# Moving work between engines and places ahead of and inside the first steps of a two-layer recurrent memory

## The reference, cut to what matters

```
k = l2norm(x_t @ Wk); v = x_t @ Wv; q = l2norm(x @ Wq)      # block 1: a memory that learns
for t in 16 steps:                                          # x_t: the 4x16 tokens of image row t
    g = grad of mean((mlp(params, k) - v)**2)               # mlp: h + gelu(h @ w1) @ w2, twice
    mom = eta * mom - lr * g
    params = params * (1 - forget) + mom                    # eta, lr, forget: means of sigmoids of x_t
out = mlp(mean over batch of params, q)                     # the read-out
y = sum over top-2 experts of weight * (gelu(ln(x) * ln_g[e] @ W1[e]) @ W2[e])   # block 2, 8 experts
A[..., 16i:16i+16] = conv1x1(A, w1) + b1, four times        # block 3, its first chain ("conv-1")
h, c = lstm step over 256 tokens                            # block 4
```

## Time and profile before

| what | value |
|---|---|
| median of the runs | 546.06 us |
| the profiled execution | 546.64 us, its span 544.8 us |
| PE busy | 476.3 us (87%) |
| DVE busy | 293.7 us (54%) |
| ACT busy | 224.3 us (41%) |
| POOL busy | 99.8 us (18%) |
| mean granted clock of PE | 0.986 |

### The profile page before, as it was taken

The page is one execution under the profiler, slowest core; times in us unless marked ns, Lnnn a source line. Parts: engine busy times, 40 slices in busy tenths (PEclk is TensorE's granted clock), DMA queues, the critical chain, the costliest instruction groups (busy, mean ns, idle before and its releaser), DMA issues.

```text
span 544.8 us, 11175 instructions
## 1 busy us (share of the span) xinstructions
PE 476.3 (87%) x3945; PEld 295.2 (54%) x3952; DVE 293.7 (54%) x1382; ACT 224.3 (41%) x1118; POOL 99.8 (18%) x101
## 2 busy tenths in 40 slices
PE   7899999999999998988887999778888887888886
PEld 4588888888865234855543776333333333333333
DVE  2966666666666756056556444664444444444443
ACT  2365556555525741025533344333333333333332
POOL 4287777767510000000000000000000000000000
PEclk8999999999997999999999999999999999999999
DMA  7600000000000000000000000000000000000000
GB/s 223 271 0 2 2 1 0 2 1 2 0 2 0 1 2 0 1 1 2 2 2 1 1 2 1 2 1 1 2 1 2 1 0 2 2 1 2 2 2 19
DMA packets 3081, 7.68 MB, mean 14 GB/s; under 512 B 1484, under 2 KB 2065, under 8 KB 2833
## 3 DMA queue, kind: packets, MB, share of 16 engines
q1 hardware_dynamic: 3026, 6.97, 3.8%
HBM read 6.71 MB, written 0.26 MB: 13 GB/s over the span
## 4 chain that ended last, share of the span: by engine, by line
PE 54%; DVE 22%; ACT 16%; issue 8%; DMA 0%; DVEq 0%; ACTq 0%
PE bk L700 12%; DVE bk L1491 8%; ACT gi L1050 6%; DVE mem L1494 6%; ACT bk L1054 6%; PE bk L659 6%; PE bk L340 3%; PE bk L585 2%; PE bk L508 2%; PE bk L838 2%; PE bk L603 2%; PE bk L489 2%; PE bk L467 2%; PE bk L477 2%; PE bk L392 2%
## 5 line engine op out<-in xcount | busy, mean ns | idle before, releaser
L838 PE MATMUL bk<-idle 128*64 128x512 bf16 (+1 forms) x650 | 175.7, 371 | 0.0
L700 PEld LDWEIGHTS bk<-mem,lvh 65*64 65x64 f32 x1536 | 79.9, 136 | 144.3 <-DVE mem L1494 142.5
L700 PE MATMUL bk<-mem,lvh 65*64 65x4 f32 x1536 | 102.1, 205 | 45.5 <-DVE mem L1494 45.1
L1050 ACT ACTIVATE gi<-bk 128x4 f32<-128x4 f32 x256 | 44.9, 175 | 136.7 <-PE bk L700 136.3
L1491 DVE TENSOR_TENSOR_SCAN bk<-gi 64x12 f32<-64x12 f32 x256 | 47.6, 186 | 91.1 <-ACT gi L1050 88.7
L1494 DVE SCALAR_TENSOR_TENSOR mem<-og,bk 64x4 f32<-64x4 f32 x256 | 38.5, 150 | 53.7 <-ACT bk L1054 53.7
L838 PEld LDWEIGHTS bk<-idle 128*64 128x64 bf16 x650 | 55.3, 110 | 16.1 <-issue 2.4
L1054 ACT ACTIVATE bk<-bk 64x4 f32<-64x4 f32 x256 | 36.6, 143 | 45.2 <-DVE bk L1491 45.2
L1498 DVE SCALAR_TENSOR_TENSOR gi<-mem,bk 64x4 f32<-64x4 f32 x255 | 39.1, 153 | 8.8
L1052 ACT ACTIVATE og<-bk 64x4 f32<-64x4 f32 x256 | 42.6, 167 | 0.0
L1140 DVE TENSOR_TENSOR mem<-mem,bk 128x256 f32<-128x256 f32 x64 | 27.0, 421 | 17.2 <-PE bk L385 11.4
(11 more groups left out here) (317 smaller groups left out, 743.7 us busy)
## 6 DMA issues: line engine op xcount, KB each, us to landing
cw<-in_cw SPq DMA_DIRECT2D x1, 3456.0 KB, 12.2
w<-in_w SPq DMA_DIRECT2D x1, 520.0 KB
mem<-in_memw SPq DMA_DIRECT2D x1, 512.0 KB, 3.6
w1g<-in_w1g SPq DMA_DIRECT2D x1, 512.0 KB
w<-in_w SPq DMA_DIRECT2D x1, 512.0 KB
xm<-in_xm SPq DMA_DIRECT2D x1, 256.0 KB, 2.7
xs<-in_x SPq DMA_DIRECT2D x1, 256.0 KB, 3.9
out<-xs SPq DMA_DIRECT2D x1, 256.0 KB, 2.0
```

Of the source, the lines that this page charges most:

```text
L700: return nc.tensor.matmul(bk[row:row + D, 2 * (s // CH % 2) + k, c:c + B], lvh[:, g, :], hist[:, s, :], start=False, stop=True, skip_group ...
L838: nc.tensor.matmul(bk[64:128, 1, 0:n], idle[:, 0:D], idle[:, 128:128 + n], start=True, stop=True)
L1050: nc.scalar.activation(gi[:, 2:2 + 3 * B:3], bk[:, bank, cols], ACT.Tanh).then_inc(sem("in_gate"), 1)
```

## The change

1. POOL no longer multiplies `w1g`. ACT does it in eight pieces of 128x128, one at the end of each of the steps 3 to 10.
2. On DVE the masked keys `kblk` are computed ahead of the unit queries `QV`, and the gate sums (`gsum`, `glin`) move from ahead of the loop into step 0, behind `v_sub`. There `gram` is masked ahead of the rates.
3. On PE in step 0, `a1` comes right behind `h1`; `gram` and then the gate sums come behind `a1`. The queries are transposed two tiles at a time in the steps 1 to 4, behind `grad_w10`, and ACT copies them to `qq` in front of that step's second gelu.
4. The three products of the conv-1 chain and their copies move to the read-out; with them the two groups of fillers in the front shrink from five to two and from five to three.
5. POOL's `k_rows(0)` moves behind the first rate products; blocks 4 to 7 go into the steps 1 to 4.

The diff, cut to its core:

```
-            pool.wait_ge(sem("ld_w1"), 64)
-            nc.gpsimd.tensor_tensor(w1g[:, :, :], w1g[:, :, :], wide(lng[:, :], 128), ALU.mult).then_inc(sem("w1g"), 1)
...
-            k_rows(0)
...
-            for n in range(1, NT):
+            for n in range(4):
                 k_rows(n)
...
+                if t <= 4:
+                    k_rows(t + 3)
...
-            nc.tensor.matmul(bk[0:D + 1, 0, 0:D + 1], c1p[:, 2, :], c1last[:, :], start=True, stop=True).then_inc(sem("c1_ps"), 1)
-            busy(5, 1)
...
+            busy(2, 1)
             pe.wait_ge(sem("KK"), 1)
...
-            busy(5, 3)
+            busy(3, 3)
...
+                if 1 <= t <= 4:
                     pe.wait_ge(sem("QV"), 1)
+                    if t == 1:
+                        pe.wait_ge(sem("rates"), 1)
+                    else:
+                        pe.wait_ge(sem("qq"), t - 1)
+                    for n in range(2):
+                        ins = nc.tensor.transpose(bk[:, 7, 256 + n * 128:384 + n * 128], QV[:, 2 * t - 2 + n, :], ident)
+                    ins.then_inc(sem("qqT_ps"), 1)
...
+            nc.tensor.matmul(bk[0:D + 1, 2, 0:D + 1], c1p[:, 2, :], c1last[:, :], start=True, stop=True).then_inc(sem("c1_ps"), 1)
             pe.wait_ge(sem("FW"), 4)
...
+            pe.wait_ge(sem("c1"), 1)
+            nc.tensor.matmul(bk[0:D + 1, 3, 0:D + 1], c1p[:, 1, :], c1a[:, :], start=True, stop=True).then_inc(sem("c1_ps"), 1)
             pe.wait_ge(sem("ld_w1"), 64)
...
+            pe.wait_ge(sem("c1"), 2)
+            nc.tensor.matmul(bk[0:D + 1, 2, 0:D + 1], c1p[:, 0, :], c1b[:, :], start=True, stop=True).then_inc(sem("c1_ps"), 1)
             busy(AFTER[1], 7)
...
+                if 1 <= t <= 4:
+                    act.wait_ge(sem("qqT_ps"), t)
+                    nc.scalar.copy(qq[:, :].rearrange("p (b t c) -> p t b c", b=B, t=T)[:, 4 * t - 4:4 * t, :, :],
+                                   bk[:, 7, 256:512].rearrange("p (t b c) -> p t b c", t=4, b=B)).then_inc(sem("qq"), 1)
                 act.wait_ge(sem("a1"), t + 1)
...
+                if 3 <= t < 3 + E:
+                    e = t - 3
+                    if e == 0:
+                        act.wait_ge(sem("ld_w1"), 64)
+                    ins = nc.scalar.activation(w1g[:, e, :], w1g[:, e, :], ACT.Copy, scale=lng[:, e:e + 1])
...
             table(ACT.Sqrt)
+            act.wait_ge(sem("c1_ps"), 2)
+            nc.scalar.copy(c1b[:, :], bk[0:D + 1, 3, 0:D + 1]).then_inc(sem("c1"), 1)
             root(2)
...
+            inverse(1, 1)
+            unit(KK[:, :, 0:D], 1)
+            unit(KK[:, :, D:2 * D], 1).then_inc(sem("KK"), 1)
+            inverse(2, 0)
             dve.wait_ge(sem("ld_id"), 16)
...
+            unit(QV[:, :, 0:D], 0)
+            unit(QV[:, :, D:2 * D], 0).then_inc(sem("QV"), 1)
```

More of the change, by code:

```diff
@@ L327, in _ @@
             pool.wait_ge(sem("f_y"), 2)
-            pool.wait_ge(sem("w1g"), 1)
             nc.gpsimd.memset(W3, 0.0).then_inc(sem("zeros3"), 1)
@@ L376, in _ @@
             pe.wait_ge(sem("gS"), 2)
-            nc.tensor.matmul(bk[0:D + 1, 2, 0:D + 1], c1p[:, 0, :], c1b[:, :], start=True, stop=True).then_inc(sem("c1_ps"), 1)
-            busy(5, 3)
+            busy(3, 3)
             def grad_w11(t):
@@ L458, in _ @@
                 else:
-                    pe.wait_ge(sem("qq"), 2)
+                    pe.wait_ge(sem("vneg"), 2)
+                    pe.wait_ge(sem("QV"), 1)
+                    for n in range(NT):
+                        w = min(128, (T - 1 - 2 * n) * TB)
+                        ins = nc.tensor.matmul(bk[:, 6 - n // 4, n % 4 * 128:n % 4 * 128 + w], kblk[:, n * 128:(n + 1) * 128],
+                                               kblk[:, (2 * n + 1) * TB:(2 * n + 1) * TB + w], start=True, stop=True)
+                        if n % 4 == 3:
+                            ins.then_inc(sem("gram_ps"), 1)
+                    pe.wait_ge(sem("ld_g"), 32)
+                    pe.wait_ge(sem("glin"), 1)
+                    for g in range(3):
+                        ins = nc.tensor.matmul(bk[:, 7, 256 + g * B * T:256 + (g + 1) * B * T], gsel[:, g, :], glin[:, :],
+                                               start=True, stop=True)
+                    ins.then_inc(sem("gate_ps"), 1)
                 for p in range(2):
@@ L566, in _ @@
             ins.then_inc(sem("logit_ps"), 1)
+            pe.wait_ge(sem("c1"), 3)
             pe.wait_ge(sem("XT"), 2)
@@ L575, in _ @@
             pe.wait_ge(sem("x2A"), 2)
+            pe.wait_ge(sem("w1g"), 1)
             pe.wait_ge(sem("ld_w2"), 32)
@@ L931, in _ @@
                     ins.then_inc(sem("R1"), 1)
+                if 3 <= t < 3 + E:
[3 more added lines that the diff above has]
+                    ins = nc.scalar.activation(w1g[:, e, :], w1g[:, e, :], ACT.Copy, scale=lng[:, e:e + 1])
+                    if e == E - 1:
+                        ins.then_inc(sem("w1g"), 1)
             for n in range(2):
@@ L942, in _ @@
             nc.scalar.copy(b1p[:, :], bk[:, 4, 0:E * HC]).then_inc(sem("b1p"), 1)
+            act.wait_ge(sem("c1_ps"), 3)
+            nc.scalar.copy(c1a[:, :], bk[0:D + 1, 2, 0:D + 1]).then_inc(sem("c1"), 1)
             root(3)
@@ L1168, in _ @@
                 if t == 0:
+                    dve.wait_ge(sem("ld_g"), 32)
+                    dve.wait_ge(sem("gS"), 2)
+                    link(nc.vector.tensor_reduce(gsum[:, :], gS[:, :].rearrange("p (s c) -> p s c", c=C), AX, ALU.add))
+                    nc.vector.tensor_scalar(glin[:, :], gsum[:, :], gaff[:, 0:1], gaff[:, 1:2], ALU.mult, ALU.add).then_inc(sem("glin"), 1)
+                    for n in range(2):
+                        dve.wait_ge(sem("gram_ps"), n + 1)
+                        nc.vector.tensor_tensor(gram[:, 8 * n + 1:8 * n + 9 - n, :],
+                                                bk[:, 6 - n, 0:(8 - n) * TB].rearrange("p (t c) -> p t c", c=TB), mid(mg, 8 - n),
+                                                ALU.mult).then_inc(sem("gram"), 1)
                     dve.wait_ge(sem("gate_ps"), 1)
@@ L1184, in _ @@
                     ins.then_inc(sem("lr"), 1)
-                    for n in range(2):
-                        dve.wait_ge(sem("gram_ps"), n + 1)
-                        nc.vector.tensor_tensor(gram[:, 8 * n + 1:8 * n + 9 - n, :],
-                                                bk[:, 6 - n, 0:(8 - n) * TB].rearrange("p (t c) -> p t c", c=TB), mid(mg, 8 - n),
-                                                ALU.mult).then_inc(sem("gram"), 1)
                 dve.wait_ge(sem("q0"), t + 1)
```

49 lines of the change are left out of this document (6 added, 43 removed).

## The result

| | before | changed |
|---|---|---|
| median of ten runs each | 546.33 us | 550.24 us |
| lowest to highest | 545.37 to 549.75 | 547.17 to 551.42 |
| profiled execution, its span | 546.64, 544.8 us | 551.08, 549.3 us |
| mean granted clock in it | 0.986 | 0.975 |

The changed kernel is slower: ratio 1.0056, 95% interval 1.0032 to 1.008. The forecast was 545.9 with an upper end of 547.8. Executions of one kernel differ by some us, and they differ with the mean clock: among 23 runs of the kernel before beside the first experiments, those at 0.985 to 0.99 took 545.9 to 548.0 us, those at 0.969 to 0.973 took 552.0 to 553.6.

A forecast was written before the change was run, and what follows sets the result against it. No engine alone bounds it, but the wait ending last in each place (PE 54% of the chain). Step 0 -1.2 to -1.5, steps 1 to 4 +1.0, read-out +0.15: middle -0.2, median forecast 545.9 us, range 543.5 to 547.8.

The forecast's parts named there:

- I take **+0.15** in all: Read-out: first conv-1 product +0.12 on PE's chain, the other two and their copies 0 to 0.15 more.
- the forecast's own signs of being wrong: Masked keys later than 20 us, steps 1 to 4 as long as the others, or steps 3 to 10 growing 0.3 us.
- Front: Up to the masked keys: clamp 1.36 to 0.17 us, masked keys complete at 19.15 in place of 21.84.
- Step 0's chain: Step 0 up to the masked prediction: it starts near 27.9 in place of 30.30, with PE at 2.4 GHz.
- the -2.4: Step 0: masked prediction 2.4 us earlier than the profiled 30.30, if PE runs at 2.4 GHz.
- The gain of the front thus passes, and nothing is added: Step 0: the front's 2.69 us carries through as -2.4; DVE's longer chain refills the wait freed by removed transposes.
- `kblk` ahead of `QV` (-1.20): Front on DVE: the masked keys start where `QV` started, 19.36 in place of 20.56, 1.20 us earlier.
- the forecast -1.2 to -1.5: End of step 0: 1.2 to 1.5 us earlier, with one stretch of about 3 us at 1.2 GHz.
- Step 0's clock: Step 0: one stretch of about 3 us at 1.2 GHz, on `gram` (-1.2, not -2.4) or the back part (0.9 lost).
- The rival "slower than before": Step 0: PE at 1.2 GHz in `gram` and again in the back part; sum +0.85, 546.9 us, chance 0.22.
- Steps 1 to 4: Two query transposes a step on PE paid in full, 0.23 each step: +1.0 us (0.9 to 1.4).
- What costs nothing: `w1g` pieces on ACT in idle time before the first gelu, and `k_rows` within POOL's waits: no cost.

The follow-up runs named there:

- run 3: Changed kernel with the conv-1 chain taken out of the read-out and put into PE's wait of step 0: 550.96 us, ratio 1.008.
- run 1: Changed kernel with the `w1g` multiplication back on POOL ahead of the loop: 549.94 us, ratio 1.0051.
- run 10: Changed kernel with ten fillers in PE's wait of step 0, and 16 fillers replacing the left-out `b1p` products in the read-out: 544.49 us, ratio 0.9924.
- run 2: Changed kernel with the query transposes in steps 5 to 8 in place of 1 to 4: 554.13 us in a single execution.
- 6: Changed kernel with the `b1p` products left out of the read-out and 16 fillers in their place: 547.94 us, ratio 0.9961.
- 7: Kernel before with the `b1p` products left out of the read-out and 16 fillers in their place: 545.23 us, ratio 0.9944.
- 9: Changed kernel with ten fillers in step 0 where PE waits 2.50 us for DVE: 547.79 us, ratio 1.0011.
- run 12: Kernel before with the `b1p` products of experts 4 to 7 behind the expert weights' transposes, 8 fillers for them: 546.97 us, ratio 0.9974.
- 13: Changed kernel with ten fillers in step 0's wait, two `b1p` products in each of steps 5 to 12, 16 fillers in the read-out: 549.19 us, ratio 1.0035.
- 14: Kernel before with two `b1p` products in each of steps 5 to 12 and 16 fillers in the read-out: 548.74 us, ratio 1.0.
- 15: Changed kernel, ten step-0 fillers; `b1p` products at the loop's end and behind the expert weights' transposes, 16 read-out fillers: 546.98 us, ratio 1.0013.
- 16: Kernel before with `b1p` products at the loop's end and behind the expert weights' transposes, 16 read-out fillers: 547.13 us, ratio 1.0.
- run 4: Kernel before with only the conv-1 chain, three products and copies, moved to the read-out: 551.76 us, ratio 1.0068.
- run 8: Changed kernel with the `b1p` products moved into PE's wait of step 0 and 16 fillers in their place in the read-out: 551.95 us, ratio 1.0031.

## Why the prediction was wrong

The step that failed is the read-out: "I take **+0.15** in all". It priced three products in PE's instruction time and never asked for the clock in that place. It measured +4.15, and run 3, with PE's old read-out and the same 17 us at 1.2 GHz, has 3.79 of it: nearly all is the clock, about 17 us at 1.2 GHz in place of 7. The profile before already showed the two short stretches there; I had read the windows of step 0 alone. None of the forecast's own signs of being wrong looked at the read-out, and none of them came true.

- **Front**: right. Clamp 0.17 us, masked keys at 18.93 for 19.15. That DVE stands behind POOL's product is shown by run 1.
- **Step 0's chain**: right as a mechanism. `gram` ran at 2.4 GHz and the masked prediction came at 27.51 (27.9). But the -2.4 set a step at 2.4 GHz against the 30.30 of an execution whose `gram` ran at 1.2 GHz. At equal clock and from the same reduce the gain is 0.71. "The gain of the front thus passes, and nothing is added" is wrong, since DVE is last at the masked prediction in both kernels and has the same operations ahead of it; `kblk` ahead of `QV` (-1.20) gains nothing there, and the stalls beside POOL are most of what is left. The step's end at -0.39, of which 0.35 lies ahead of the change, is further from the forecast -1.2 to -1.5 than it looks.
- **Step 0's clock**: the place was named ("PE stands idle for some 2 us that it spent on transposes before"), the size wrong: about 7 us at 1.2 GHz, not 3. From the masked prediction to the next gelu the changed kernel took 7.18 and run 10 4.78 (26.61 to 31.39): 2.4 us lost, not 0.9. The six profiles with and the six without fillers show that the empty wait is the cause. The rival "slower than before" had the 1.2 GHz in `gram` as well, which didn't happen in this execution (it did in run 2), and ended at 546.9 for lack of the read-out.
- **Steps 1 to 4**: +0.66, not +1.0; run 2 shows that it is the transposes.
- **What costs nothing**: right for `w1g` on ACT and for `k_rows`.

The terms close: -0.39 by the first gelu of step 1, +0.66, +4.15 make 4.42, the difference of the spans (549.27 less 544.85). That they close is arithmetic; that the front's 0.35 fell to the changed kernel is luck.

**Shown**: the loss in the read-out is time at 1.2 GHz (the table); fillers in place of the one-column products end the long stretch (6, 7); the empty wait costs step 0 its clock (9, 10); at equal clock the change is worth next to nothing by the loop's end (10 with 12, 13 with 14, 15 with 16). **Not settled**: why the changed kernel meets the long stretch more often. The read-out's products are the same, and the kernel before meets it too: 24 of its 156 executions beside the experiments had a mean clock of 0.976 or less (552.0 us or more) and 64 one of 0.977 to 0.984 (546.4 to 549.9), against 6 of 10 at 0.976 or less of the changed kernel, all 6 of run 3, which has PE's old read-out, and 5 of 9 of run 4, which has the old front. In the eight profiles with all products in the read-out, the stretch is long (10 to 20 us in all) in the seven where the clock falls 1.2 to 2.8 us after the first product of `b1p`, so while they run, and short in the one where it falls 4.1 us after it, behind them (the kernel before). Where it falls differs between executions; that the changed timing shifts the odds is a reading of one profile for each kernel, and run 1, with the changed read-out and a later start, had only 1 of 12 executions so low. Which place for the products would keep the clock up in a complete kernel stays open too.

## What to carry to other kernels

Read the granted clock in every stage that a change touches or delays, not only where work is removed, and price an edit on PE at both levels. An engine freed from work in a wait leaves that wait empty; here the empty wait cost 2.4 us of step 0, more than the 0.71 that the change gains in it. Before two executions are compared, look for the first row that the change can touch and count from there: here that turned 1.25 us into 0.04. And a result within one per cent needs several executions of each kernel with their clocks beside them before it can be read as a gain or a loss of the code.

## What the runs showed of the hardware

- PE can be busy 2.00 of 2 us on products of one column (0.12 us a row, 4.45 us for 32) and be put to 1.2 GHz all the same, for 17 us; between 160 and 175 us its longest wait was 0.22. The Trainium skill (TensorE: Matmul & The Clock Gate, section "HAM oscillation") traces such falls to PE's waits for data; the fall of step 0 came in a wait (2.50 us, for DVE and not for a DMA), the read-out's did not.
- At 1.2 GHz a place loses far less than half: 0.28 to 0.38 us for each us in the read-out, where the chain runs over other engines too. The 32 rows of products themselves take 3.68 us at 2.4 GHz (the kernel before, whose clock falls behind them), 4.45 where it falls among them (the changed kernel) and 6.83 at 1.2 GHz (run 8).
- A DVE operation of 0.17 us can take 1.85 beside POOL (run 1); in step 0 a copy of 128x16 (L1199) takes 0.95 beside POOL's first rate product, before 0.93 (L1181); a product that reads a bank keeps its 0.22 beside the second one.
- Executions differ ahead of the first step too: the transposes of the input took 1.03 us in run 10 and 1.89 in run 12, and DVE's first reduce came 1.21 us apart.
